# Counting a third of the edge tiles by one-hot products, and scattering the codes of the others

## The reference

```python
x = layernorm(x + x + mlp(segment_sum(edge_attr, dst)))             # layer 0
x = layernorm(x + (x@Ws.T + bs + (segment_sum(x[src]*ew, dst)
                   / max(segment_sum(ew, dst), 1)) @ Wn.T + bn)/2)  # layer 1
x = layernorm(x + relu(x@w_s + segment_sum((x@w_n)[src], dst)))     # layer 2
x = layernorm(x + cheb(relu(cheb(x, G1, gb1)), G2, gb2))            # layer 3
# in cheb: deg[n] = number of edges with src == n and src != dst
#          w[e] = -deg[src]**-0.5 * deg[dst]**-0.5  (0 where src == dst)
```

## Time and profile before

| | us |
|---|---|
| time, median of 3 runs | 4458.62 (4454.08 to 4461.81) |
| profiled execution, its own time | 4466.06 |
| its span, first to last instruction | 4464.0 |
| busy: TensorE matmuls, weight loads | 3560.5, 2728.0 |
| busy: VectorE, ScalarE, GpSimd | 3173.4, 2444.6, 3007.1 |

### The profile page before, as it was taken

One profiled execution on the slowest core, in us unless ns is written; L12 is line 12 of the kernel. 1 busy time (PEld: TensorE's weight loads), 2 busy tenths in 40 slices (PEclk: granted clock), 3 DMA queues, 4 the chain that ended last, 5 costly groups with the idle time before them and its releaser, 6 DMA issues. The chain is left out here.

```text
span 4464.0 us, 77093 instructions
## 1 busy us (share of the span) xinstructions
PE 3560.5 (80%) x21778; PEld 2728.0 (61%) x21778; DVE 3173.4 (71%) x13414; ACT 2444.6 (55%) x7163; POOL 3007.1 (67%) x3450
## 2 busy tenths in 40 slices
PE   6868887999899999999999956566898989931111
PEld 3336655766588888888888746565455768831111
DVE  8988876677588888888888868788222446655555
ACT  0006665666588888888888856311565764421111
POOL 0006656555388888888888767576775757767777
PEclk9989997888899999999999978888999999965555
DMA  0015643444222222222222235454676987843332
GB/s 19 1 45 155 166 133 127 164 166 167 100 77 77 77 76 77 76 76 76 77 77 77 68 123 156 127 157 143 221 247 217 310 288 247 260 140 93 98 94 77
DMA packets 307439, 575.11 MB, mean 129 GB/s; under 512 B 65310, under 2 KB 93783, under 8 KB 307018
## 3 DMA queue, kind: packets, MB, share of 16 engines
q1 hardware_dynamic: 234890, 442.75, 29.4%
q0 software_dynamic: 72128, 127.43, 10.9%
HBM read 300.83 MB, written 270.68 MB: 128 GB/s over the span
## 5 line engine op out<-in xcount | busy, mean ns | idle before, releaser
L1316 PE MATMUL ps<-ident,rows 128*128 128x128 f32 x1372 | 280.9, 310 | 605.2 <-ACT rows L1093 498.3
L540 POOL DMA_INDIRECT rows<-state,rows_of_src x588 | 557.4, 948 | 252.6 <-issue 171.7
L1093 ACT ACTIVATE rows<-rows,lap_w 128x128 f32<-128x128 f32 (+1 forms) x784 | 270.7, 419 | 607.3 <-DMA rows<-lap,rows_of_lap 480.0
L1316 PEld LDWEIGHTS ps<-ident,rows 128*128 128x128 f32 x1372 | 191.4, 159 | 672.7 <-ACT rows L1093 453.6
L810 DVE TENSOR_TENSOR_SCAN x<-same,x,ps 128x512 f32<-128x512 uint8 x336 | 429.0, 1277 | 236.5 <-PE ps L1316 204.6
L1076 ACT ACTIVATE yTa<-ps 128x512 f32<-128x512 f32 x392 | 233.5, 596 | 607.8 <-PE ps L1298 607.6
L540 POOL DMA_INDIRECT rows<-lap,rows_of_lap x392 | 390.5, 996 | 168.5 <-issue 117.1
L618 POOL DMA_INDIRECT lk<-node_table,look_idx x392 | 384.6, 981 | 92.1 <-issue 83.6
L575 POOL TENSOR_TENSOR y<-xin,c0h 128x512 f32<-128x512 f32 x245 | 310.8, 1269 | 200.0 <-DVE outb L982 142.6
L926 DVE BATCH_NORM_STATS2 bn<-y 128x6 f32<-128x128 f32 x1764 | 378.6, 276 | 42.8 <-POOL y L575 42.7
L1454 PE MATMUL ps<-V,hT 128*128 128x128 f32 x3136 | 402.0, 281 | 5.5 <-ACT hT L1206 5.5
(11 more groups left out here) (253 smaller groups left out, 9601.1 us busy)
## 6 DMA issues: line engine op xcount, KB each, us to landing
state_h<-hb SPq DMA_DIRECT2D x98, 512.0 KB, 3.9
xin<-in_x_dram SPq DMA_DIRECT2D x196, 256.0 KB, 2.8
out_dram<-outb SPq DMA_DIRECT2D x196, 256.0 KB, 2.1
xe<-state SPq DMA_DIRECT2D x147, 256.0 KB
state<-outb SPq DMA_DIRECT2D x98, 256.0 KB, 2.1
state<-oe SPq DMA_DIRECT2D x98, 256.0 KB, 2.1
h_pre<-hb SPq DMA_DIRECT2D x49, 512.0 KB, 3.1
rows<-in_edge_attr_10x_dram SPq DMA_DIRECT2D x48, 320.0 KB, 3.2
```

Source lines behind the costliest of these rows:

```text
L540: gp.indirect_dma_start(out=dest[:, at, k, 0:width], out_offset=None, in_=table_, in_offset=bass.IndirectOffsetOnAxis(ap=index[:, c:c + 1] ...
L1316: i = t.transpose(bank(g.b)[:, k, :], rows[:, g.r, k, 0:P], ident[:, :])
```

## The change

Tiles whose number is a multiple of three (66, `COUNTED`) are counted as before. For the other 130 (`PUT`) only the degree is counted: `bin_s`, `lane_s` and two matmuls. Their codes are computed by VectorE for all edges at once (`put_code`, with the row in `put_row`; edges that aren't last get a row outside the table, which the scatter drops), and GpSimd scatters them, one indirect DMA of 128 single words a tile, into a DRAM table `node_put` that SyncE has filled with zeros. SyncE waits for all 130, reads the table back into SBUF (`put_back`, in the buffer `hT`), and VectorE adds it to the code column.

```diff
+        node_put = dram("node_put", (P * BINS, 1))
...
+        put_row, put_code, look_f = cols(outb, 3, I32), cols(outb, 4), cols(y1, 4)
+        put_back = hT[:].rearrange("p a k d -> p (a k d)")[:, 0:BINS]
...
+        COUNTED = [c for c in range(TILES) if c % 3 == 0]
+        PUT = [c for c in range(TILES) if c % 3 != 0]
...
@@ SyncE
             sp.wait_ge(fixed, 1)
+            sp.dma_start(node_put.rearrange("(p n) c -> p (n c)", p=P), put_back).then_inc(put_zeroed, 16)
             sp.dma_start(lap1[SLOTS:SLOTS + P, :], zeros[:, :]).then_inc(tables_st, 16)
             sp.dma_start(lap2[SLOTS:SLOTS + P, :], zeros[:, :]).then_inc(tables_st, 16)
+            sp.wait_ge(code_put, 16 * len(PUT))
+            sp.dma_start(put_back, node_put.rearrange("(p n) c -> p (n c)", p=P)).then_inc(codes_in, 16)
             sp.wait_ge(vstep, V_TABLE)
...
@@ GpSimd
+            gp.memset(put_back, 0.0)
...
+            pool.wait_ge(put_zeroed, 16)
+            pool.wait_ge(vstep, V_COLS)
+            for c in PUT:
+                gp.indirect_dma_start(out=node_put, in_=put_code[:, c:c + 1], in_offset=None, bounds_check=P * BINS - 1,
+                                      oob_is_err=False,
+                                      out_offset=bass.IndirectOffsetOnAxis(ap=put_row[:, c:c + 1], axis=0))\
+                    .then_inc(code_put, 16)
             leave(pool)
...
@@ VectorE
+            v.scalar_tensor_tensor(put_code, v_tile, float(P), v_lane, ALU.mult, ALU.add)
+            link(v.tensor_copy(look_f, look_idx[:, :, 1]))
+            v.tensor_tensor(put_row, t_f, look_f, ALU.add)
...
                 v.tensor_scalar(bin_s, iota_bin, a_src[:, c], None, ALU.is_equal)
-                v.tensor_scalar(bin_d, iota_bin, a_dst[:, c], None, ALU.is_equal)
-                v.tensor_scalar(lane_s, iota_lane, b_src[:, c], mask[:, c], ALU.is_equal, ALU.mult)
-                v.tensor_scalar(lane_t, iota_lane, b_dst[:, c], v_tile[:, c], ALU.is_equal, ALU.mult)
-                v.tensor_scalar(lane_l, iota_lane, b_dst[:, c], v_lane[:, c], ALU.is_equal, ALU.mult)\
-                    .then_inc(hots, 1)
+                i = v.tensor_scalar(lane_s, iota_lane, b_src[:, c], mask[:, c], ALU.is_equal, ALU.mult)
+                if g.c in COUNTED:
+                    v.tensor_scalar(bin_d, iota_bin, a_dst[:, c], None, ALU.is_equal)
+                    v.tensor_scalar(lane_t, iota_lane, b_dst[:, c], v_tile[:, c], ALU.is_equal, ALU.mult)
+                    i = v.tensor_scalar(lane_l, iota_lane, b_dst[:, c], v_lane[:, c], ALU.is_equal, ALU.mult)
+                i.then_inc(hots, 1)
...
             link(v.reciprocal(flat(x3)[:, 0:BINS], flat(x3)[:, 0:BINS]))
+            dve.wait_ge(codes_in, 16)
+            v.tensor_tensor(table[:, :, 0], table[:, :, 0], put_back, ALU.add)
...
@@ TensorE
                 for bk, lanes, bins in ((0, lane_s, bin_s), (2, lane_t, bin_d), (4, lane_l, bin_d)):
+                    if bk and g.c not in COUNTED:
+                        continue
+                    first, last = (g.c == c for c in ((COUNTED[0], COUNTED[-1]) if bk else (0, TILES - 1)))
```

More of the change, by code:

```diff
@@ L279, in gnn_kernel @@
                              "alink", "dlink", "roots_in", "hots", "counted"))
-        edges_in, as_float, listed, lanes_made = (sem(n) for n in ("edges_in", "as_float", "listed", "lanes_made"))
+        edges_in, as_float, listed, put_zeroed, code_put, codes_in = (
+            sem(n) for n in ("edges_in", "as_float", "listed", "put_zeroed", "code_put", "codes_in"))
         seam, padded = sem("seam"), sem("padded")
@@ L1269, in count_tile @@
             def count_tile(g):
-                first, last = (g.c == c for c in (0, TILES - 1))
                 pe.wait_ge(hots, g.lin(1, 1))
```

## The result

| | before | changed kernel | ratio |
|---|---|---|---|
| median (lowest to highest), us | 4457.76 (4454.08 to 4461.81) | 4400.91 (4398.10 to 4403.89) | 0.9872 [0.9855, 0.9889] |
| profiled execution, its own time | 4466.06 | 4398.87 | |
| its span | 4464.0 | 4396.8 | |
| from the start to the first seam | 310.9 | 261.6 | |

The changed kernel is 1.3% faster, 56.9 us by the medians; 39.3 were forecast. That is this chip. On another the same kernel is 2.3% slower than before; the experiments come to that.

What follows compares the result with a forecast made beforehand. Bound taken: the edge counting, where TensorE and VectorE are tied by two buffer sets. Sum: 4466.1 - 49.3 (counting) + 1.0 (operations ahead) + 8 (contention) + 1.0 (addition) = 4426.8, or 4419 us on the median; range 4386 to 4449.

Steps and rivals of the forecast that it cites:

- the tie: Counting: VectorE waits until TensorE frees one of two one-hot buffer sets, 2.70 us; full, short, short take 3.26 us.
- Rival (1): Counting: VectorE alone sets the pace, without waiting for TensorE; 4372 us, chance 0.08.
- Counting 217 us: Edge counting ahead of the first pass: 213 us of groups plus 4 for the opening, against 266.5 before.
- The opening: First tiles of the counting: TensorE's matmuls at half pace cost about 4 us more than before.
- The three operations ahead: Before the counting: three more VectorE operations over 196 columns, +0.96 us on the path.
- the addition: After the counting: one more VectorE tensor_tensor over 782 columns adds the codes, 0.97 us.
- Scatters hidden: Beside the counting: 130 GpSimd scatters at 1.30 us, codes back by 200 us, wanted at about 266.
- Rival (2): Counting: shared port lets GpSimd issue only in VectorE's pauses; slower, 4486 us, chance 0.07 together with very late landing.
- rival (3): Counting: TensorE stays at the low clock, 1.2 GHz, a group taking 4.32 us; slower, 4482 us, chance 0.06.
- Contention 8 us: Counting: each scatter issue costs VectorE 0.1 us, about 58% on the path; 8 us, between 0 and 20.
- The passes behind are the same work: Passes after the first seam: start earlier by the preamble's difference, 39 us, with unchanged lengths.
- the signs that it gave for the scatters: Counting: 130 indirect issues of about 1.0 us ending near 195 us, and no wait for the codes.

Runs made afterwards that it cites:

- e6: Changed kernel with all 66 full tiles first and its scatters left out (codes missing): 4361.87 us, ratio 0.9787 to before.
- e7: Changed kernel with three sets of one-hot buffers instead of two and its scatters left out (codes missing): 4374.46 us, ratio 0.9808 to before.
- e4: Changed kernel without its 130 scatters (codes missing), on a chip with before at 4743.02 us: 4686.09 us, ratio 0.9881.
- e11: Changed kernel with each scatter issued only when the one two before has landed, on a chip with before at 4739.78 us: 4699.19 us, ratio 0.9918.
- e5: Changed kernel again, nothing edited, on a chip with before at 4463.06 us: 4402.27 us, ratio 0.9875.
- e8: Changed kernel again, nothing edited, on a chip with before at 4736.72 us: 4845.54 us, ratio 1.0228.
- e3: Kernel before with three sets of one-hot buffers instead of two, on a chip with before at 4743.02 us: 4737.85 us, ratio 0.9989.
- e1: Changed kernel with all 66 full tiles first, scatters kept, on a chip with before at 4743.02 us: 4798.43 us, ratio 1.0125.
- e12: Changed kernel with all 66 full tiles first, scatters back to back, on a chip with before at 4739.78 us: 4808.29 us, ratio 1.0138.

## Why the prediction was right, point by point

The measured 4400.9 us lies 18 below the forecast 4419, inside the stated range (4386 to 4449) and below the forecast's own (4405 to 4432). The mechanism, a counting paced by the tie and scatters hidden behind it, is what this chip's runs show. The faster time than forecast comes from two terms that were taken too high, and from passes behind that no term had.

- **The tie, 2.70 us and a group of 3.26: right.** 3.27 in the order of time, the wait 0.71 (0.79 forecast), 47.4 us over 65 groups. Rival (1), VectorE alone, is refuted by that wait; e6 and e7 show its room: 42 and 36 us that an order or a third buffer set would give.
- **Counting 217 us: 215.1.** The opening cost 1.2 us, not 4: the thirteenth tile starts 14.26 us after the first, where four groups of 3.257 are 13.03. The saving written down, 49.3, should have been 266.5 - 217 = 49.5. The three operations ahead (start of the counting at 24.91 instead of 23.67: 1.2 us, forecast 1.0) and the addition (0.98, and 0.89 to the next start) came as worked out.
- **Scatters hidden, 1.00 + 0.30 us each: right.** 992 ns in the median, started until 197.3, landing 2.2; nobody waits for the codes. Rival (2), and the rule of the Trainium skill (SBUF — State Buffer, "Who interferes with whom") by which a tensor_scalar that holds the shared ports keeps GpSimd's descriptors from being written, did not come about: the issues lie beside tensor_scalars all through the stretch, and the longest took 1122 ns. Whether these tensor_scalars ran in the two-port modes of that rule, no run shows. The granted clock was 1.00, so rival (3) did not either.
- **Contention 8 us: this term was mis-sized; it came to about 0.9.** Both of its factors were too high. All one-hots together last 216.9 us with the scatters and 211.9 without (e4, on the slower kind, same instructions, same clock), so an issue costs 0.04 us of VectorE's instructions, not 0.1. And of these 5.0 us only 0.9 is on the path, 18% and not 58%: a group takes 3.271 us against 3.257, all of it in the making of the full tile (1.436 against 1.423). The lengthened instruction is mostly a narrow one (L750's group 355 ns, L747's 319, where undisturbed ones are 307 and 308), and the next starts as soon after it as ever, 0.23 us in both traces:

```profile
102.30 0.39 DVE L750 TENSOR_SCALAR hb<-y 128x128 f16<-128x128 f16 x1
102.53 0.30 DVE L751 TENSOR_SCALAR hb<-y 128x128 f16<-128x128 f16 x1
```

The countings as a whole, 215.1 us and 215.3, are equal by chance, since e4's opening is 1 us slower. In e11 wide one-hots lengthen too, and about 8 us come through, so that the term's size was not unreasonable, only not this chip's.
- **"The passes behind are the same work": true of the work, not of the time.** 49.3 of 56.9 us are the preamble. The other 7.6 were in no term. Whether they belong to the change stays open. On the first kind of chip all four runs gain behind the seam as well (7.6, and in e5, e6 and e7 11.3, 10.0 and 2.8), and `src0` takes 495 to 498 us in all four against 507.9; on the other kind the sign varies (e4 gains 7.4, e8 loses 10.3). `src0` goes with TensorE's granted clock: 0.85 and 0.86 where it takes 495 to 500 us, 0.82 and 0.83 where it takes 507 to 512 (before and e3, but also the changed kernel in e8). What sets the clock there was not tested.
- Of the 18 us between 4419 and 4400.9, some 7 are thus the contention, 3 the opening, and nearly 8 the passes behind. The preamble alone moved by 49.3 us where the terms gave 39.3; that 49.3 is also the figure written for the counting's saving is chance, since the counting saved 51.4 (266.5 - 215.1) and the two other terms took 2 of it back.
- **What it did not see at all:** that on another chip TensorE's increments come late while the same scatters are issued. In e8 the signs that it gave for the scatters all read "right" (issues of 0.97 us that end at 194, no wait for the codes), but the counting ends at 387.4, and the clock of 0.51 in the stretch would have pointed to rival (3), of which it is not the cause: a tile's matmuls are 1 us longer by it, a group 25. The trace of before, taken on a chip of the first kind, could not show it.

## What to carry to other kernels

Two engines that hand buffers back and forth are bound by the time from one buffer's making to its return; when tiles become unequal, put equal ones together or add a set before counting on the faster engine's own pace. That GpSimd's queue is idle doesn't make work free there. Time a long run of small indirect DMAs on more than one chip, and try pacing it: in e11, on one chip, waiting for the one two before took the preamble to 269.2 us, where it was 409.3 unpaced on another of its kind. A gain of 1% that rests on 196 handovers of 0.1 us (0.06 there, 0.04 back) is lost at once if the way back takes 10 to 30.

## What the runs showed of the hardware that was not expected

- On three chips (those of e1, e8 and e12), while GpSimd issues 128-descriptor indirect scatters every 1.30 us, TensorE's semaphore increments come late in the counting: in e1 VectorE starts a tile up to 30 us after the matmuls that free its buffers (134.01 to 163.99). VectorE's own increments are on time (0.01 us, TensorE starting 0.06 after the one-hots). At one scatter in 1.54 us (e11), and with none (e4), TensorE's are on time too. In the first measurement and on the chip of e5 they lag 0.01 to 0.02 us at 1.33. The scatters themselves land as usual: in e8 SyncE reads the table at 195.31, after a last issue at 193.14. Why is not settled.
- The same three chips are slower in the edge passes in all kernels: `L1`, `L2`, `T1`, `T2`, `LH`, `LU` took 327, 312, 315, 318, 322 and 563 us in e8, against 271, 262, 279, 273, 262 and 525 in the changed kernel's first trace, while `tgt0` (361 and 360) and `nodes` (1401 in both), which have gathers too, agree. It doesn't need this change: e3 (before with a third set) and e4 (no scatters in the preamble) show it as well (`L1` 331 and 324 us). Their traces show late increments of TensorE there. In `L1`, 64 of 134 recorded ones in e3 and 73 of 126 in e4 come over 0.1 us behind the end of TensorE's last instruction that updates the semaphore, the longest 11 us; in before and in the changed kernel's first trace none of 146 and 147 does. Those of ScalarE and VectorE are on time in that pass; in the last, which scatters as well, some of VectorE's are late too (66 in e4). In `nodes` some of TensorE's are late by up to 0.9 us (70 of 494 between 1400 and 1900 us in e8), and the pass is no longer for it. Whether the late increments are all that makes the edge passes slower was not tested.
